# The state-space mixer's normaliser sum in the gate's PSUM bank, one wait less at two exponentials, and another order of two ScalarE steps

## The reference

```python
g = y * silu(gate)                       # y: the scan's output, 4096 channels
gg = g.reshape(B, L, 8, 512)
var = mean(gg * gg, axis=-1)
gg = gg * rsqrt(var + EPS)
out = einsum('bli,di->bld', gg.reshape(B, L, 4096) * norm_weight, W_out)
```

## Time and profile before

| what | value |
|---|---|
| median of three runs | 2728.96 us (2727.36 to 2730.19) |
| the profiled execution's own time | 2725.77 us |
| its span, first to last instruction | 2723.7 us |
| mean granted TensorE clock | 0.943 |
| PE / DVE / ACT / POOL busy, share of span | 85% / 68% / 53% / 47% |
| ACT table loads at lines 988 and 999 | 126 and 128, 1283 ns each |

### The profile page before, as it was taken

The page is one execution under the profiler, slowest core; times in us unless marked ns, Lnnn a source line. Parts: engine busy times, 40 slices in busy tenths (PEclk is TensorE's granted clock), DMA queues, the critical chain, the costliest instruction groups (busy, mean ns, idle before and its releaser), DMA issues. The chain is left out here.

```text
span 2723.7 us, 45778 instructions
## 1 busy us (share of the span) xinstructions
PE 2303.1 (85%) x16164; PEld 1814.0 (67%) x16164; DVE 1864.1 (68%) x3274; ACT 1442.1 (53%) x2439; POOL 1268.8 (47%) x1250
## 2 busy tenths in 40 slices
PE   4995888898889888988898886279999998699993
PEld 3784777777777777777777775258888886444432
DVE  5875776666667666766666664667777776777765
ACT  1432777677777777777777674112222222356662
POOL 3542765665657656666567554035555542000000
PEclk9996999999999999999999998589999998799996
DMA  2002112112111111121111112010000000312214
GB/s 83 11 10 103 49 42 73 37 48 76 41 68 42 49 68 44 47 76 41 68 42 49 41 41 77 18 33 26 26 26 25 20 26 14 115 64 78 78 63 132
DMA packets 91521, 141.19 MB, mean 52 GB/s; under 512 B 23328, under 2 KB 60544, under 8 KB 90048
## 3 DMA queue, kind: packets, MB, share of 16 engines
q1 hardware_dynamic: 89280, 133.96, 14.9%
q10 hardware_dynamic: 2048, 4.72, 0.5%
HBM read 118.12 MB, written 20.32 MB: 51 GB/s over the span
## 5 line engine op out<-in xcount | busy, mean ns | idle before, releaser
L1056 DVE SCALAR_TENSOR_TENSOR mix_cv<-mix_pp,mix_cw,mix_cv 128x384 f32<-128x384 f32 (+4 forms) x864 | 491.6, 572 | 336.3 <-ACT mix_cv L983 315.8
L845 POOL TENSOR_TENSOR mix_zt<-mix_zsq 128x256 f32<-128x256 f32 x128 | 93.4, 730 | 491.9 <-ACT mix_zsq L1007 491.9
L839 POOL TENSOR_TENSOR mix_ce<-mix_ce,mix_cv 128x1024 f32<-128x1024 f32 x112 | 264.7, 2363 | 0.0
L999 ACT ACT_TABLE_LOAD x128 | 164.2, 1283 | 186.3 <-PE mix_pd L894 186.3
L1195 POOL TENSOR_TENSOR ffn_hl<-ffn_h,ffn_hh 128x512 fp32r<-128x512 f32 x112 | 144.8, 1293 | 249.8 <-ACT ffn_hh L1253 249.8
L965 PE MATMUL mix_px<-mix_wo,mix_z 128*128 128x256 f32 x1024 | 258.0, 397 | 2.9 <-ACT mix_ss L1029 2.9
L983 ACT ACTIVATE mix_cv<-mix_pp,mix_cb,mix_cw 128x384 f32<-128x384 f32 (+1 forms) x288 | 180.5, 627 | 131.9 <-PE mix_pp L77 131.9
L75 PE MATMUL mix_pp<-l0in_XH,mix_w_lo 128*128 128x384 f32 (+2 forms) x576 | 224.1, 389 | 27.5 <-DVE mix_ss L1045 21.2
L1718 DVE TENSOR_REDUCE att_tops<-att_psc 128x1 f32<-128x512 f32 (+3 forms) x384 | 189.9, 551 | 56.2 <-PE att_psc L1666 32.1
L965 PEld LDWEIGHTS mix_px<-mix_wo,mix_z 128*128 128x128 f32 x1024 | 200.8, 201 | 28.0 <-ACT mix_ss L1029 3.3
L1069 DVE SCALAR_TENSOR_TENSOR mix_py<-mix_cv,mix_dsk,mix_py 128x128 f32<-128x128 f32 x512 | 144.6, 351 | 105.2 <-PE mix_py L920 105.2
(11 more groups left out here) (330 smaller groups left out, 7117.4 us busy)
## 6 DMA issues: line engine op xcount, KB each, us to landing
mix_ce<-ecs SPq DMA_DIRECT2D x112, 512.0 KB, 3.7
mix_w_raw<-in_w_in SPq DMA_DIRECT2D x8, 1280.0 KB, 5.5
a_part<-att_sums SPq DMA_DIRECT2D x32, 256.0 KB, 5.0
ffn_raw<-in_wgu SPq DMA_DIRECT2D x56, 128.0 KB, 2.2
mix_ll<-cs SPq DMA_DIRECT2D x384, 4.0 KB
mix_wo<-in_w_out SPq DMA_DIRECT2D x8, 512.0 KB, 6.6
ffn_draw<-in_wd SPq DMA_DIRECT2D x28, 128.0 KB, 2.1
q<-qkv_part SPq DMA_DIRECT2D x24, 128.0 KB, 1.9
```

The lines of the kernel that those rows point to most:

```text
L839: pool.tensor_tensor(ce[o][:, :, :], ce[o][:, :, :], cv[:, CT_C, cols_of(c)].unsqueeze(1).to_broadcast([P, GH, Q]), ALU.mult).then_inc(ce_ ...
L999: act.activation(lm[o][:, 4 * i:4 * i + 4, :].rearrange("p h l -> p (h l)"), pd[:, :], ACT.Exp).then_inc(l_done, 1)
L1056: last = dve.scalar_tensor_tensor(out, of, cw[:, g, ct, 3 - d:4 - d], out, ALU.mult, ALU.add)
```

## The change

The sum of squares goes to column 0 of the gate's bank `pgt` instead of a column of `px`: it now waits until ACT has taken the gate (`w_done`), and the next gate waits until ACT has taken the sum (`ss_done`); the projection no longer waits for `ss_done`. On PE the last `fill` stands ahead of the sum, on ACT the last `init` ahead of `ss`. The two Exp lose their wait for `yd_done`. On ACT `init(ks[0])` stands ahead of the older blocks' Silu.

```diff
@@ gate (PE) @@
                     wait(pe, w_done, u)
+                    wait(pe, ss_done, u - 2)
@@ PE, in a slot @@
                     if len(ks) > 2:
                         fill(ks[1])
+                    if len(ks) > 1:
+                        fill(ks[-1])
                     if 0 <= p < NC:
-
+                        pe.wait_ge(zs_done, p + 1)
+                        pe.wait_ge(w_done, min(c + 2, NC))
+                        pe.matmul(pgt[:, 0:1], zs[:, :], one[:, :], start=True, stop=True).then_inc(n_done, 1)
                         pe.wait_ge(xtok_ready, min(c + 1, NC))
                         if not live:
                             pe.wait_ge(acc_done, e + 1)
-                        pe.wait_ge(zs_done, p + 1)
-                        pe.matmul(px[:, D:D + 1], zs[:, :], one[:, :], start=True, stop=True).then_inc(n_done, 1)
-                    if len(ks) > 1:
-                        fill(ks[-1])
-                    if 0 <= p < NC:
-                        pe.wait_ge(ss_done, p + 1)
-                        pe.wait_ge(z_done, p + 1)
@@ ACT, in a slot @@
                         for i in range(2):
-                            wait(act, yd_done, c - 1)
                             act.wait_ge(d_done, 2 * c + i + 1)
                             act.activation(lm[o]..., pd[:, :], ACT.Exp).then_inc(l_done, 1)
+                    if ks:
+                        init(ks[0])
                     for k in fills(c - 1)[1:]:
                         squash(k)
-                    if ks:
-                        init(ks[0])
...
+                    if len(ks) > 1:
+                        init(ks[-1])
                     if 0 <= p < NC:
                         act.wait_ge(n_done, p + 1)
                         wait(act, rs_done, p - 1)
-                        act.activation(ss[p % 2][:, :], px[:, D:D + 1], ACT.Identity, ...).then_inc(ss_done, 1)
-                    if len(ks) > 1:
-                        init(ks[-1])
+                        act.activation(ss[p % 2][:, :], pgt[:, 0:1], ACT.Identity, ...).then_inc(ss_done, 1)
```

More of the change, by code:

```diff
@@ L1028, in _ @@
                         wait(act, rs_done, p - 1)
-                        act.activation(ss[p % 2][:, :], px[:, D:D + 1], ACT.Identity, bias=eps_sum[:, 0:1]).then_inc(ss_done, 1)
-                    if len(ks) > 1:
-                        init(ks[-1])
+                        act.activation(ss[p % 2][:, :], pgt[:, 0:1], ACT.Identity, bias=eps_sum[:, 0:1]).then_inc(ss_done, 1)
             @block.vector
```

## The result

The changed kernel takes 2604.13 us (median of four runs, 2600.48 to 2619.47) against 2728.16 for the kernel before: a ratio of 0.9555 (95% interval 0.9516 to 0.9595), 124 us less. The forecast was 2597, with a range of 2560 to 2642. The highest run, 2619.47, had a mean granted clock of 0.903 where the others had 0.947; it left no trace, and I leave it unexplained. The profiled execution took 2602.0 us, against 2725.77 before.

What follows compares the result with a forecast made beforehand. It took a loop through PE, ACT and POOL around the sum of squares as the bound. Slots 121.5 us plus clock 10.5 gave 132 off 2725.8, 2594; the runs' median lies 3.2 higher: 2597, range 2560 to 2642.

Steps and rivals of the forecast that it cites:

- The load of Exp runs ahead with one wait: ACT, line 999: with one wait left, Exp's table load starts ahead of it, hidden; 186.3 us of idle stood before it.
- the load stays behind the wait: Rival at Exp's table load, line 999: the change doesn't free it, 56 us of gain lost, 2653; chance 0.06.
- The 0.37 that PE waits goes: PE at `decays(c, 1)`: its wait for the first Exp, 0.37 us a slot, disappears.
- Slot 0's 1.00: PE in slot 0 of each eight, where `py` is shorter: 1.00 us of waiting for Exp goes.
- The fill leaves the loop: PE: the last fill moves into the idle before the sum, saving 0.80 us, or 1.14 with a 384-column block.
- init(ks[0]): right in size: ACT: init ahead of the Silu delays the square of z by 0.16 us, or 0.50 with a 384-column block.
- Three-block slots: Slots 3 and 7: PE itself late, so less gain; 0.37 us in slot 7, 1.15 for both together.
- The clock: PE after slot 0's sum: shorter idle, 1.60 us, avoids some clock falls; half of 21 us taken, 10.5.
- POOL did not bind: Rival at POOL's queue before z is squared: another wait takes over and eats half of 132, 2663; chance 0.11.
- ACT's wait for the fill: Rival at ACT's init(ks[0]): waiting for the fill makes the kernel slower, some 2790 to 2890; chance 0.03.
- The waits costed at nothing: PE's new waits for `w_done` and `ss_done` of the slot before: already met when PE arrives, no cost.
- The table switch costs its record only: Rival at ACT's table loads: a drain makes each switch 2.66 us in all, time 2610 or 2609; chance 0.01.

Runs made afterwards that it cites:

- the two runs: The changed kernel with the sum back in `px` and the projection behind `ss`, 2691.98 us; the changed kernel with the last fill behind the sum, 2730.02 us.
- the run with the square ahead: The changed kernel with the `px` copy and the square of z ahead of the Silu load, older blocks' Silu behind the gate's: 2537.25 us.

## Why the prediction was right, and where it was off

- **The load of Exp runs ahead with one wait: right.** Idle 186.3 to 2.2; undone, 219.4. That line, not the rest of the change, does it. The reason given, two waits against one, is too broad: what holds the load is the wait for `d_done`, an instruction of its own ahead of it. The rival "the load stays behind the wait" is refuted.
- **What that is worth: the step that was mis-sized.** "The 0.37 that PE waits goes" should have been 0.20: 0.17 remains as idle of the weight load. In the two-block slots 1, 2 and 4 to 6 the gain is 0.80, not 1.01; 5 x 0.2 x 15.5 = 16 us. Slot 0's 1.00 was right (1.07 alone, and 1.67 measured for its whole 1.64). The 0.37 is a row of the weight loads, PEld, the 1.00 one of the matmuls, PE; in slot 0 too the weight load's row (1.24, below) is 0.17 above what went. The forecast took the idle named after Exp for idle caused by Exp; the 0.17 that remains was visible only once Exp was out of the way.
- **The fill leaves the loop: right,** 0.80 in the narrow slot. That the bank and the fill are worth little apart was in the working only in part ("that wait gave nothing by itself"); the two runs show it.
- **init(ks[0]): right in size,** 0.16 and 0.50 forecast, 0.17 and 0.51 alone. In the changed kernel the order costs 45 us in all, clock included.
- **Three-block slots:** 1.15 forecast for slots 3 and 7 together, 0.82 + 0.37 = 1.19 measured. That these agree is luck, as Exp gave 0.20 here too. In slot 7 the third fill, now right behind another, delays the sum by 0.98 (5.50 to 6.48 after `decays(c, 1)`) and not by 1.14. And DVE's earlier taps, which the forecast had put at nothing, keep PE from waiting at that fill: with the early init undone, slots 3 and 7 are 0.21 and 0.13 longer.
- **The clock: right in kind.** The idle before slot 0's sum came out at the 1.60 worked out, and 6 of 15 fell, not 13. Thirteen falls cost 24 us (two of them some 3 each), six cost 10: 14 gained, where 10.5 was taken. That half of the span came so near is luck; no row could tell it.
- **The sum.** Slots 87.4 to 80.6 per period, 6.8 x 15.5 = 106; clock 14; the ends of the mixer, the remainder, 4. Together 124 against 132 forecast: 16 too much from Exp, 4 too little from the clock, 4 from the ends. Of the stated range, the upper end of 2622 is not what its parts give: 2597 + 10.5 + 12 = 2619.5.
- **The other rivals.** POOL did not bind: it still waits for ACT in all 128 slots, 354.8 / 128 = 2.8 us each, the value that the rival left it. ACT's wait for the fill stayed below the half microsecond named: in the slot shown, init starts 0.12 behind Exp's end, in wide slots 0.46 to 0.48. The waits costed at nothing cost next to nothing: PE's matmuls wait 0.5 us for taps at a fill, once, and 3.8 us for the gate's Silu at the sum, twice, in the whole mixer.
- **The table switch costs its record only.** The next ACTIVATE starts 1.30 behind the load that starts at 937.66, and in the run with the square ahead the gate's Silu starts 1.29 behind its load (905.89). The Trainium skill's page ScalarE: Activation LUTs, section What ACT_TABLE_LOAD costs, adds a drain of about 1380 ns; the traces of all these kernels disagree.

The weight load of the kernel before at the `decays` of the earlier trace rows:

```profile
1077.16 0.11 PEld L894 LDWEIGHTS mix_pd<-mix_rl,mix_ll 96*128 96x128 bf16 x2 [1.24 <-ACT mix_lm L999]
```

Two slot 0s of the changed kernel, PE, for the clock:

```profile
352.25 0.38 PE L956 MATMUL mix_pgt<-mix_one,mix_zs 128*128 128x1 f32 x2 [1.60 <-POOL mix_zs L848]
352.49 3.39 PE L963 MATMUL mix_px<-mix_wo,mix_z 128*128 128x256 f32 x8
...
357.28 0.39 PE L895 MATMUL mix_pd<-mix_rl,mix_ll 96*128 96x256 bf16 x2
...
1003.37 0.38 PE L956 MATMUL mix_pgt<-mix_one,mix_zs 128*128 128x1 f32 x2 [1.61 <-POOL mix_zs L848]
1003.61 1.97 PE L963 MATMUL mix_px<-mix_wo,mix_z 128*128 128x256 f32 x8
...
1006.76 0.39 PE L895 MATMUL mix_pd<-mix_rl,mix_ll 96*128 96x256 bf16 x2
```

The same idle to 0.01 us, and once the projection takes 3.39, once 1.97; from sum to `decays(c, 1)` 5.03 against 3.39.

Open: what the 0.17 us at the weight load of `decays` is; whether the two waits of Exp in the other order, with `d_done` carried by Exp, would free the load as well (not run).

## What to carry to other kernels

When an engine waits for another at a point, take off only what the next limit behind it leaves: undo the wait in one run and look what idle stays in that place. Measure the loss by the starts of the matmuls; the idle of a weight load overstated it here. Look at each activation with a table load for waits that stand ahead of the load as instructions of their own, and put what needs no load ahead of it. Two edits that each cover the other's wait (a bank of its own, and the work moved out of the gap) are worth costing together and alone.

## What the runs showed of the hardware

- **The clock after a gap is not certain either way.** PE's idle before the sum of slot 0, and the falls in 15 slots: 2.75 us (early init alone), 15; 2.68 (fill behind the sum), 8; 2.24 (kernel before), 13; 2.18 (one wait alone), 10; 1.60 (changed kernel), 6; 1.61 (sum in px, and one wait undone), 8 each; 1.03 (init undone), none. Slot 4 with 1.71 (fill behind the sum): 10; with 1.80 (early init alone): 1. So the idle alone does not decide it. Two sums of slot 0 with the fill behind the sum:

```profile
446.03 0.38 PE L954 MATMUL mix_pgt<-mix_one,mix_zs 128*128 128x1 f32 x2 [2.68 <-POOL mix_zs L848]
...
536.88 0.38 PE L954 MATMUL mix_pgt<-mix_one,mix_zs 128*128 128x1 f32 x2 [2.68 <-POOL mix_zs L848]
```

The granted clock of the 3.5 us behind the first is 0.65, behind the second 1.00. A fall mostly costs about 1.6 us, by the granted clock at a mixture of 1.2 and 2.4 GHz (0.56 in the changed kernel).

- **A load runs ahead of the wait that its activation carries, not of one that stands ahead as an instruction of its own:** six kernels with one wait at Exp have 2.2 to 2.3 us of idle before 128 loads; three with two waits, of which `d_done` stands alone, have 186.3, 201.7 (early init alone) and 219.4. The gate's Silu in the last run has two waits and 2.3 us before 127 loads, as the one that stands alone was met.
